# A landing wait at every fourth row gather of a graph network kernel

## The reference

```python
# first network
h   = einsum('ni,hio->nho', x, W_att)                      # 4 heads
e   = leaky_relu(<h[src], a_src> + <h[dst], a_dst>, 0.2)
out = segment_sum(segment_softmax(e, dst) * h[src], dst).mean(heads)
g   = x;  twice: g = segment_sum(g[src], dst) / degree     # two hops
x   = x + concat(out, g @ W_g + b_g) @ W_w + b_w
# second network, 5 layers
h   = leaky(x @ W1 + b1) @ W2 + b2
e   = leaky(edge_attr @ We1 + be1) @ We2 + be2
agg = segment_sum(h[src] * e * dot_scale, dst)
x   = layernorm(x + agg * res_w) * ln_g + ln_b
```

## Time and profile before

| | |
|---|---|
| time, median of 3 runs | 8059.58 us (8065.32, 8059.58, 8028.11) |
| span of the profiled execution | 8041.5 us; no time of its own is given beside it |
| busy: PE, DVE, POOL, ACT | 70%, 60%, 52%, 50% |
| DMA | 103 GB/s on the mean, 828.41 MB |
| row gathers by POOL (L693) | 4016, of them 556 in the hop pass, 808 in the attention pass, 2652 in the layers |

### The profile page before, as it was taken

How to read it: one execution, slowest core, us unless ns; L and a number is a source line. 1 busy time by engine, 2 the same in 40 slices (tenths; PEclk the granted TensorE clock), 3 DMA queues, 4 the chain that set the end, 5 groups by cost and what they waited for, 6 DMA issues and landing times.

```text
span 8041.5 us, 131647 instructions
## 1 busy us (share of the span) xinstructions
PE 5609.6 (70%) x48820; PEld 4901.3 (61%) x48820; DVE 4833.5 (60%) x12225; ACT 3995.4 (50%) x6886; POOL 4208.7 (52%) x4251
## 2 busy tenths in 40 slices
PE   6787772333333788876788877888867888688886
PEld 5676651222222677776777766777757777577776
DVE  5565565566575566655666665566656666566666
ACT  3454444555564355553555544555535555355554
POOL 4454457666665355554555544555545555455554
PEclk8898775655555788887888887888878888689887
DMA  3333325767675233332233322323323333233322
GB/s 85 83 96 83 84 72 174 233 233 240 233 259 198 52 79 80 83 79 57 80 84 79 82 71 67 79 80 84 81 57 80 84 83 79 56 79 83 83 80 68
DMA packets 509356, 828.41 MB, mean 103 GB/s; under 512 B 112942, under 2 KB 220069, under 8 KB 495662
## 3 DMA queue, kind: packets, MB, share of 16 engines
q1 hardware_dynamic: 373374, 650.98, 24.0%
q0 software_dynamic: 135344, 169.01, 11.5%
HBM read 385.16 MB, written 434.48 MB: 102 GB/s over the span
## 4 chain that ended last, share of the span: by engine, by line
PE 36%; issue 12%; DVE 12%; another core or an unknown queue 7%; POOL 1%; ACT 1%; DMA 0%; DVEq 0%; SPq 0%; POOLq 0%; ACTq 0%
PE psum L1354 30%; DVE arena L1756 5%; PE psum L1368 5%; DVE by_lane L1819 2%; DVE psum L1802 1%; DVE es_w L1756 1%; POOL agg L700 1%; DVE gring L1796 0%; DVE psum L1808 0%; PE psum L1280 0%; PE psum L1311 0%; DVE xin L1756 0%; DVE gring L1756 0%; DMA agg<-rowsg,last_i 0%
## 5 line engine op out<-in xcount | busy, mean ns | idle before, releaser
L693 POOL DMA_INDIRECT gring<-tableh,src_i x2652 | 2600.3, 980 | 2529.9 <-DVE psum L1802 1560.1
L1354 PE MATMUL psum<-penalty,arena 125*128 125x192 bf16 x24736 | 2659.8, 260 | 611.6 <-issue 579.9
L1354 PEld LDWEIGHTS psum<-penalty,arena 125*128 125x128 bf16 x24736 | 2232.7, 103 | 859.3 <-issue 789.4
L693 POOL DMA_INDIRECT gring<-table,src_i x1364 | 1388.7, 1018 | 1031.9 <-issue 402.7
L1756 DVE TENSOR_SCALAR arena<-dst_f,node_id 125x640 bf16<-125x640 f16 x4556 | 1605.1, 401 | 0.1
L1796 DVE TENSOR_REDUCE gring<-psum 128x128 f32<-128x384 f32 x505 | 355.9, 705 | 1996.9 <-remote 1286.4
L967 ACT COPY psum<-diag 128x512 f32<-128x512 f32 x505 | 297.5, 590 | 2355.9 <-DVE psum L1802 2202.9
L1368 PE MATMUL psum<-arena 128*128 128x128 f32 x4040 | 706.3, 311 | 180.1 <-issue 164.8
L1368 PEld LDWEIGHTS psum<-arena 128*128 128x128 f32 x4040 | 601.2, 218 | 243.7 <-issue 241.8
L1486 DVE SCALAR_TENSOR_TENSOR arena<-psum,be_c,arena 128x512 f32<-128x512 f32 x505 | 376.7, 746 | 450.5 <-ACT arena L839 260.1
L839 ACT ACTIVATE arena<-psum,be_leak 128x512 f32<-128x512 f32 x505 | 335.9, 686 | 602.3 <-remote 410.6
(11 more groups left out here) (271 smaller groups left out, 7681.2 us busy)
## 6 DMA issues: line engine op xcount, KB each, us to landing
rows<-arena SPq DMA_DIRECT2D x101, 1296.0 KB
acts<-arena SPq DMA_DIRECT2D x505, 256.0 KB
arena<-acts SPq DMA_DIRECT2D x505, 256.0 KB
rowsg<-run SPq DMA_DIRECT2D x505, 256.0 KB
gring<-tableh,src_i POOLq DMA_INDIRECT x2652
dst_f<-pe_src SPq DMA_DIRECT2D x430, 93.8 KB
rows<-run SPq DMA_DIRECT2D x101, 256.0 KB
gring<-table,src_i POOLq DMA_INDIRECT x1364
```

What stands on the lines that cost most here:

```text
L693: pool.indirect_dma_start(ring[:, s, k, :], None, table, bass.IndirectOffsetOnAxis(ap=src_i[:, c * K + k:c * K + k + 1], axis=0))\
L1354: ins = mm(found(n)[:, m, :], hot_at(n // 2, j)[:, at:at + P], parts[:, j, :, :].rearrange("q a f -> q (a f)"), start=(j == 0), stop=(j == ...
```

## The change

A counter runs over all row gathers of all passes, at build time. Behind every fourth one POOL gets a wait for the semaphore of the ring slot, with the value that this slot has when all its gathers so far have landed. `sent` holds these values by slot and starts anew with each semaphore set: once for the hop pass, once for the attention pass, once for the five layers. Nothing else is changed; `gather_nodes` has no such wait.

```diff
+BURST = 4
...
-            def gather_chunk(c, s, table, ring, ready, cols):
+            issued = [0]
+
+            def gather_chunk(c, s, table, ring, ready, sent, cols):
                 for k in range(cols):
                     pool.indirect_dma_start(ring[:, s, k, :], None, table,
                                             bass.IndirectOffsetOnAxis(ap=src_i[:, c * K + k:c * K + k + 1], axis=0))\
                         .then_inc(ready[s], 16)
+                    sent[s] += 16
+                    issued[0] += 1
+                    if issued[0] % BURST == 0:
+                        pool.wait_ge(ready[s], sent[s])
...
+            sent = [0] * SL
             for c in range(CH):
...
-                gather_chunk(c, c % SL, table1, gather1, g1_ready, K - k1(c))
+                gather_chunk(c, c % SL, table1, gather1, g1_ready, sent, K - k1(c))
...
-                gather_chunk(c, c % SL, table2, gather2, g2_ready, K)
+                gather_chunk(c, c % SL, table2, gather2, g2_ready, sent, K)
...
-                    gather_chunk(c, n % SL, tableh, gatherg, gg_ready, K - kp(n))
+                    gather_chunk(c, n % SL, tableh, gatherg, gg_ready, sent, K - kp(n))
```

## The result

The changed kernel takes 8130.83 us (median of 4 runs, 8111.7 to 8137.36), the kernel before beside it on the same chip 8062.45 us (4 runs, 8028.11 to 8078.08). The ratio is 1.0109, with a 95% interval of 1.0067 to 1.0151: 68 us slower. The profiled execution took 8136.76 us, 93.5 us of span more than before.

A forecast was written before the change was run, and what follows sets the result against it. No engine was busy over 70% and POOL's gathers set nothing; POOL would bound only the attention pass. Span 8041.5 + 282 there + 0 for hop pass and layers = 8324, forecast as 8335 us between two bases, range 8155 to 8540.

The forecast's parts named there:

- Attention pass: Attention pass: POOL becomes the bound, slot waits vanish, 201 pauses of 2.8 us; the pass costs +282 us.
- The price of a pause: POOL behind every fourth gather: landing about 2.2 plus restart 0.6, so 2.8 us, between 1.43 and 4.25.
- quiet price: Pause of POOL for a landing when all is quiet: taken as 2.0 us, between 1.43 and 2.22.
- +121 us for the pass: Rival in the attention pass: gathers land as when quiet, pause 2.0 us; total 8163 us, chance 0.14.
- Hop pass and layers: I cost the waits at nothing: Hop pass and five layers: POOL's slack covers the pauses, so the waits add 0 us.
- the prediction's own limit: Pause length from which POOL becomes the bound: 2.57 us in layer 1, 2.75 in layer 0, about 3 in hop pass.
- the layers become POOL-bound too: Rival in layers and hop pass: pauses of 3.0 us exceed POOL's slack, +272 us, total 8596; chance 0.11.
- Faster: Rival at PE's lookup matmuls: breaking up gather bursts recovers two thirds of 579.9 us issue idle, total 7936; chance 0.04.
- 2.5 to 3.1 us, some 200 times: Sign in the attention pass: POOL's idle before gathers is put down to DMA, with this length and count.
- The pass some 1600 us and 57%: Sign: the attention pass lengthens to some 1600 us and its DMA share falls from 69% to about 57%.
- The layers keep their length within 1%: Sign in the layers: length unchanged within 1%, while POOL's slot waits on DVE shrink from 323.5 us in layer 0.
- I am wrong if the lookups' issue time changes by more than a tenth: Refuting sign at PE's lookup matmuls: their 579.9 us of issue idle should stay within a tenth.

The follow-up runs named there:

- b_only_att: Kernel before plus the landing wait behind every fourth gather in the attention pass only, chip A: 6268.69 us, 1.095 of the kernel before.
- d_memset2: Kernel before plus five small POOL memsets behind every fourth gather in hop pass and layers, no landing wait, chip D: 7234.36 us, 0.8774.
- b8_not_att: Kernel before plus a landing wait behind every eighth gather in hop pass and layers, none in the attention pass, chip C: 7694.94 us, 0.9494.
- b16_not_att: Kernel before plus a landing wait behind every sixteenth gather in hop pass and layers, none in the attention pass, chip D: 8169.75 us, 0.9908.
- e_passed: Kernel before plus one always-met POOL wait per chunk, behind its fourth gather, in hop pass and layers, chip A: 5720.86 us, 0.9999.
- e_passed2: Kernel before plus one always-met POOL wait per chunk, behind its fourth gather, in hop pass and layers, chip E: 8070.66 us, 0.9983.
- memset3: Kernel before plus three small POOL memsets behind every fourth gather in hop pass and layers, no landing wait, chip E: 7329.26 us, 0.9054.

## Why the prediction was right and wrong

**Attention pass: right, a little small.** The mechanism held in each part: POOL is the bound, slot waits are gone, the DMA share is 0.57 as forecast, and the last gather ends after 780.9 + 835.7 = 1616.6 us of POOL's time against 1593.3 forecast. Two errors partly cancel: gathers take 0.966 us each in place of 1.050 (68 us less in all), and the pause is 3.19 us in place of 2.8 (+78). The pass costs +304 in place of +282; "b_only_att" shows, on chip A, that the waits there do nothing else.

**The price of a pause.** My quiet price of 2.0 us (at most 2.22) is 2.58 in the layers, and 2.8 is 3.19 in the attention pass. The "at most" was no bound: it was made of a landing seen at the kernel's end, at its quietest, and of one restart. The Trainium skill (DMA: Bandwidth & Descriptors, "Anatomy of one DMA — SWDGE (gpsimd) path") gave 2.0 us fixed plus bytes, which the prediction turned into a pause of 2.0 and +121 us for the pass; this trace disagrees, with 3.19 and +304. The same page's "Latency and other measured facts", by which the memory's latency is longer at high load, fits in kind: 2.58 us at a share of 0.31, 3.19 at 0.57, though the rows are twice as long there too.

**"Hop pass and layers: I cost the waits at nothing": this step failed.** It put the term of these passes at 0, since POOL's slack covers the pauses and all else stays. Neither held. By the prediction's own limit, 2.57 us in layer 1, a pause of 2.58 uses up the slack, and POOL became the bound. That is the rival "the layers become POOL-bound too", right in its mechanism (chance 0.11; its sum charged the hop pass 14 us at a pause of 3.0, though the limit there, (1101 - 665) / 139, is 3.14). But the pass that POOL now bounds is not the pass of before: the limits were worked out from a layer of 970 us that itself held slow issue, and without it the rest of the kernel would go faster than 970 us. "d_memset2", at 883 to 889 us a layer, shows this. The term that I priced at 0 measured -213 us in the first trace (-62 hop, -151 layers), and -271 by the medians on chip C.

**"Faster", chance 0.04: its mechanism was there, and decided the size.** I had the earlier trace rows and named that gathers starve PE and that breaking them up would help, then dismissed it with "PE also runs at full pace at times under gathers, and the number of gathers is the same". The number is the same, but the length of the unbroken run is not, and "b8_not_att" (0.949), "b16_not_att" (0.991) and the memsets show that the run and the stop are what count. (The 1.08 us that it read as the distance of single matmuls is the idle time before each; their starts in the earlier trace rows lie 1.44 us apart.) It should have been a term of the sum beside the +282, as large as POOL's new bound leaves it: 100 chunks at POOL's 9.6 us in place of 970 to 994 us a layer. In the later runs on chips B and D the same changed kernel was faster than before by 2.2 and 1.4%, so the sign of the forecast holds for the chip of the result and not for those.

**The signs I named.** Pauses in the attention pass "2.5 to 3.1 us, some 200 times": 198, at 3.19. The pass some 1600 us and 57%: 1635 (1617 in the stretch) and 57%. "The layers keep their length within 1%": no, -2.6 to -4%. "I am wrong if the lookups' issue time changes by more than a tenth": it did, and this sign pointed at the right place.

**What stays open.** Why unbroken gathers slow PE's issue is not shown. It needs neither a low clock nor contention that the DMA share shows (0.13 at the layer's start), and it doesn't need landing waits to go. What distinguishes chip A, where 16 matmuls take 1.48 us beside the same gathers, is not settled. One difference stands in the traces themselves. The gathers of a run raise their semaphores in 64256 steps (4016 gathers of 16). The trace of "e_passed" on chip A holds 63498 of them; that of the kernel before holds 16966, of "e_passed2" 16505, of "memset3" 18400, of the changed kernel 37799. So the traces of the chips with slow issue also lack many of these records, and the names that the profile gives to what ended a wait ("issue", "remote") are weaker there. Every timed execution here has a recorded span and clock, so whether PE's issue would be slow without recording is a rival that no run tests.

## What to carry to other kernels

A wait is not only a cost: before pricing added waits at nothing because an engine has slack, ask what its unbroken stream does to the others, and treat unexplained "issue" time on the bounding engine (580 us here) as a term with its own bound, not as background. A slack worked out from the present length of a pass is good only while what sets that length stays. If a stream of gathers must be broken up, a short stop of known length (1.8 us: 0.877) beats waiting for a landing (2.6 us: 0.968); where the stream is not in the way, as on chip A, every stop is a loss (1.211 and 1.318); and it is to be left out of passes that the gathers bound (+304 us in the attention pass); and a change of 1% is to be measured on more than one chip, since here the same two kernels gave 1.011, 0.978 and 0.986.

## What the hardware showed that was not expected

One kernel has two speeds by chip: 5723 us on chip A, 8062 to 8256 on the others. In layer 1 the difference is PE's idle time (8 us against 180, mostly slow issue) and its busy time for the same matmuls (660 us at a granted clock of 1.00 against 790 at 0.89). With slow issue single matmuls start about 0.7 us or twice that apart (1.41 us from 3782.69 to 3784.10 in the first trace, at a granted clock of 1.00; 1.42, 1.39 and 0.71 at 3798 to 3802 us, at 0.50). A met wait on POOL costs nothing (0.9999 and 0.9983), a landing wait 2.58 us of POOL when the DMA engines are a third busy and 3.19 us when they are at 57% and the rows are twice as long.
